# A shared-expert split moved one attention step on, and three neighbours of it reordered, in an attention and mixture-of-experts kernel

## The chip, the cores and the metric

The kernel runs on one core of a Trainium2 chip. The metric is device time in microseconds (us), lower is better. The five engines are TensorE (PE in the rows; PEld is its weight load), VectorE (DVE), ScalarE (ACT), GpSimd (POOL) and SyncE (SP, which here only issues DMAs).

## The reference

One layer of linear attention with decay over 4096 tokens of width 512, a layer norm, then a mixture of 64 experts (top 6, at most 128 slots each) plus one shared expert, and a second layer norm:

```python
q, k, v = split(x @ w_qkv);  q, k = elu(q) + 1, elu(k) + 1
running_kv, running_ksum = decay_scan(k * v), decay_scan(k)      # s = decay * s + x over the tokens
x1 = layernorm(x + (q * running_kv / sum(q * running_ksum)) @ w_out)
scores = softmax(x1 @ gate_w.T);  w, e = top_k(scores, 6)
routed = sum over the chosen experts of w * ((silu(g) * u) @ down_proj[e]),  g, u = split(x1 @ gate_up_proj[e])
shared = silu(x1 @ shared_gate_w.T) * (x1 @ shared_up_w.T) @ shared_down_w.T
out = layernorm(x1 + routed + shared)
```

Every float32 factor is written as a high part (rounded, made by ScalarE) and a low part (the rest, made by VectorE as the difference), and TensorE computes three products for one.

## The kernel before

**Attention.** The tokens are cut into eight blocks of 512 (`it`), and each block takes four steps (`c`), one for each 128 of the width. Every engine runs its own list of the same steps, written out by hand, and semaphores join them. In a step (it, c) TensorE projects k, v and q, ScalarE makes the exponentials and relus (`e`, `relu`), VectorE makes `phi_k`, the two scans `run_k` and `run_kv`, `phi_q` and `qk`. Mixed in is the work of the block before: four quotients (`spread` on TensorE, `divide` on VectorE, `split_att` for their high and low parts), four `out_rows` (the output projection, one for each 128-token tile), `add_x1` with the norm's statistics (`mv`), three small GpSimd instructions for the norm (`norm`), and `apply_x1` on ScalarE. A later step turns the tile (`turn_x1`, `copy_turned`), computes its gate logits, picks the top six (`top`, `route`, `place`) and, on GpSimd, writes the tile's slots with six indirect DMAs (`scatter`). Tiles 24 to 27 get their output rows in block 7; the tiles from `LAST` = 28 on get theirs in a tail after the last step. Tiles up to 26 are scattered, the last five are counted into the table by matmuls (`table_add`).

**The shared expert** is cut into units of one chain of matmuls each (gate, up, then pairs of down rows); the first run in the tail, the others between the experts and behind them. Before the first unit its operands must be split: the turned x1 of block 0 (`split_x1t(0)`: four casts `x1t_hi` on ScalarE, four differences `x1t_lo` on VectorE, from `x1t_stage`, which SyncE loads in step (7, 0)), the up weights (`su_hi`, `su_lo`), the gate weights (`sg_hi`, `sg_lo`) and the down weights (`sd_hi`, `sd_lo`). The semaphore `shared_split` counts the low parts that are ready; the down units and two expert loads of SyncE wait for its last value.

**What sets the order** around the change is the written order of each engine's list. An engine that waits holds up everything behind it in its own list.

Of the kernel before, what the change touches and what calls it, by code (L numbers as in the profile page):

```python
# [7 lines left out]
F32 = mybir.dt.float32  # L8
# [3 lines left out]
ALU = mybir.AluOpType  # L12
# [33 lines left out]
def build(nc, x, x_t, w_qkv, w_out, decay_param, gate_t, w_gu, w_down, sg_t, su_t, sd_t, out):  # L46
# [5 lines left out]
    NB = T // BT  # L52
    NJ = BT // P
    NT = T // P
    KC = D // P
    SC = SI // P
# [264 lines left out]
    with ExitStack() as ctx:  # L321
# [93 lines left out]
        def _(sp):  # L415
# [151 lines left out]
            store_turned(LAST - 1)  # L567
            load_xres(NB - 1, 3)
            store_score(LAST - 1)
            sp.wait_ge(shared_split, 3)  # L570
            for e in range(2):
                load_down(e)
            for i in range(LAST, NT):
# [59 lines left out]
        def _(act):  # L633
# [112 lines left out]
            def unit():  # L746
                b, part = divmod(unit_at[0], UNITS)
                unit_at[0] += 1
                if part < 2 * SC:
                    c = part // 2  # L750
                    n = SC * b + c
                    if part % 2 == 0:
                        act.wait_ge(g_mm, n + 1)
                        if n:
                            act.wait_ge(silu_done, n)
                        ps = proj_ps[(unit_take(b) + part) % 3]
                        act.activation(tanh_s[:, :], ps[:, :], ACT.Tanh, scale=0.5).then_inc(tanh_done, 1)
                        if part == 0 and b + 1 < NB:
                            load_x1t(b + 1)
                    else:  # L760
                        act.wait_ge(hid_s_done, n + 1)
                        if b:
                            act.wait_ge(down_mm, NJ * b)
                        act.copy(hid_hi[:, c, :], hid_s[:, :]).then_inc(hid_hi_done, 1)
                    return
                if part == 2 * SC and b + 1 < NB:
                    split_x1t(b + 1)
                pair = part - 2 * SC
                for j in (2 * pair, 2 * pair + 1) if b < EARLY else ():
                    act.wait_ge(down_mm, NJ * b + j + 1)  # L770
                    if b == 0 and j == 0:
                        act.wait_ge(heads_mm, NB)
                    if b == 1 and j == 0:
                        act.wait_ge(rest_mm, NT)
                        act.wait_ge(out_mm, NT)
                        act.wait_ge(table_done, TABLE_JOINED)
                    if b >= len(shared_rows) and j == 0:
                        act.wait_ge(shared_out[b - len(shared_rows)], 16)
                    act.copy(shared_rows[b % len(shared_rows)][:, j, :], proj_ps[rows_take[b, j] % 3][:, :]).then_inc(rows_copied, 1)
# [48 lines left out]
            for it in range(NB):  # L828
                for c in range(KC):
                    step(it, c)  # L830
                    if (it, c) == (NB - 1, 0):
                        split_x1t(0)
                    if (it, c) == (NB - 1, 1):
                        split_shared(0, "u", su_hi, su_stage)
                    if (it, c) == (NB - 1, 2):
                        split_shared(1, "g", sg_hi, sg_stage)
# [11 lines left out]
            divided[0] += 2  # L848
            split_att()
            copy_logits(LAST - 2)  # L850
            unit()
            divided[0] += 2
            split_att()
            scale_score(LAST - 2)
            unit()
            apply_x1(LAST - 1)
            unit()
# [108 lines left out]
        def _(dve):  # L966
# [286 lines left out]
            def split_shared(hi, lo, view):  # L1253
                dve.tensor_tensor(lo[:, :, :], view[:, :, :], hi[:, :, :].bitcast(F32), ALU.subtract).then_inc(shared_split, 1)

            def step(it, c):
                tile, before_tile = tile_of(it, c), tile_of(it, c - 1)
                s = it * KC + c
# [4 lines left out]
                    numerator(s - 1)  # L1263
                if s and it + 1 < NB:
                    x_low(it + 1, c)
                dve.wait_ge(phi_parts, 2 * s + 1)
                if s:
                    dve.wait_ge(run_kv_done, s)
# [36 lines left out]
                mix(it, c, 1)  # L1305
                if c == 0 and it:
                    rden_low(it - 1)
                if (it, c) == (NB - 1, KC - 2):
                    dve.wait_ge(shared_hi_done, 1)
                    split_shared(su_hi, su_lo, su_stage)  # L1310
                if (it, c) == (NB - 1, KC - 1):
                    dve.wait_ge(shared_hi_done, 2)
                    split_shared(sg_hi, sg_lo, sg_stage)
# [46 lines left out]
            divide(NB - 1, 1)  # L1360
            place(LAST - 3)
            split_att()
            top(LAST - 2)
            route(LAST - 2)
            unit()
            divide(NB - 1, 2)
            divide(NB - 1, 3)
            split_att()
            place(LAST - 2)
            unit()  # L1370
            add_x1(LAST)
            unit()
            dve.wait_ge(shared_hi_done, 3)
            split_shared(sd_hi, sd_lo, sd_stage)
            add_x1(LAST + 1)
            top(LAST - 1)
            route(LAST - 1)
            add_x1(LAST + 2)
            place(LAST - 1)
            add_x1(LAST + 3)  # L1380
# [244 lines left out]
        def _(pe):  # L1625
# [123 lines left out]
            def unit():  # L1749
                b, part = divmod(unit_at[0], UNITS)  # L1750
                unit_at[0] += 1
                if part < 2 * SC:
                    c = part // 2
                    take = unit_take(b) + part
                    cols = slice(c * P, (c + 1) * P)
                    w_hi, w_lo = (su_hi, su_lo) if part % 2 else (sg_hi, sg_lo)
                    pe.wait_ge(shared_split, 2)
                    pe.wait_ge(x1t_lo_done, KC * (b + 1))
                    pe.wait_ge(*freed[take - 3])
                    products = []  # L1760
                    for k in range(KC):
                        products += three(w_hi[:, k, cols], w_lo[:, k, cols], x1t_hi[:, k, :], x1t_lo[:, k, :])
                    chain(proj_ps[take % 3][:, :], products).then_inc(u_mm if part % 2 else g_mm, 1)
                    return
                pair = (2 * (part - 2 * SC), 2 * (part - 2 * SC) + 1)
                pe.wait_ge(shared_split, 3)
                for late_chunk in (False, True):
                    for j in pair:
                        take = rows_take[b, j]
                        tok = slice(j * P, (j + 1) * P)  # L1770
                        chunks = [SC - 1] if late_chunk else range(SC - 1)
                        if not late_chunk:
                            pe.wait_ge(*freed[take - 3])
                        pe.wait_ge(hid_lo_done, SC * b + (SC if late_chunk else SC - 1))
                        products = []
                        for c in chunks:
                            products += three(hid_hi[:, c, tok], hid_lo[:, c, tok], sd_hi[:, c, :], sd_lo[:, c, :])
                        mm = chain(proj_ps[take % 3][:, :], products, first=not late_chunk, final=late_chunk)
                        if late_chunk:
                            mm.then_inc(down_mm, 1)  # L1780
# [150 lines left out]
```

## Time and profile before

| | |
|---|---|
| three runs | 949.8, 950.09, 954.65 us (median 950.09) |
| profiled execution | 952.04 us, its span 949.6 us |
| PE busy | 919.3 us, 97% of the span |
| DVE, ACT, POOL busy | 683.2, 499.7, 463.9 us |
| mean granted TensorE clock | 0.993 |

Busy time is an average over the whole span; the attention steps end near 411 us, the tail runs to about 475 us, the experts follow up to about 880 us and the last norm closes the kernel. Times in the rows count from the start of the span, so a row of one engine can be laid beside a row of another.

### The profile page before, as it was taken

What the parts mean: (1) busy time and instruction counts of PE and PEld (TensorE: products, weight loads), DVE (VectorE), ACT (ScalarE), POOL (GpSimd) and SP (SyncE); (2) the same over time, 40 slices, a digit from 0 to 9 for tenths busy, and PEclk for the clock granted to TensorE, in tenths of its full rate; (3) what the DMA queues carried; (4) which work ended last, traced back from release to release, by engine and by line L of the source; (5) the groups of instructions that cost most, each with busy time, mean ns of one, the idle gap of its engine ahead of it and who ended that gap; (6) DMA issues with size and microseconds to landing.
All of it is one profiled execution on the core that took longest, in us unless ns stands there. A gap on an engine that the chain in (4) does not pass through costs nothing. (4 is left out here: it accounts for less than half of the span.)

```text
span 949.6 us, 15173 instructions
## 1 busy us (share of the span) xinstructions
PE 919.3 (97%) x4626; PEld 728.9 (77%) x4626; DVE 683.2 (72%) x1248; ACT 499.7 (53%) x1015; POOL 463.9 (49%) x540
## 2 busy tenths in 40 slices
PE   8999999999999998998999999999989999999996
PEld 7788888878887886786787767777767777777875
DVE  7996878889797975887776556575656665636776
ACT  5543535344443433443556655666645666545775
POOL 2002456665656654577135455554454644433564
PEclk9999999999999998999999999999999999999999
DMA  6244635334343515176569999999999999969972
GB/s 209 88 154 122 176 87 166 108 115 124 126 126 92 157 59 184 55 239 222 167 201 298 304 321 312 321 314 308 312 303 300 320 319 302 319 116 392 385 255 112
DMA packets 114190, 203.91 MB, mean 215 GB/s; under 512 B 18496, under 2 KB 56384, under 8 KB 113088
## 3 DMA queue, kind: packets, MB, share of 16 engines
q1 hardware_dynamic: 93584, 159.87, 51.0%
q0 software_dynamic: 19520, 35.75, 16.4%
q10 hardware_dynamic: 1008, 7.34, 2.1%
q8 instruction: 38, 0.62, 0.3%
q14 instruction: 40, 0.33, 0.1%
HBM read 143.03 MB, written 59.88 MB: 214 GB/s over the span
## 5 line engine op out<-in xcount | busy, mean ns | idle before, releaser
L1531 POOL DMA_INDIRECT slot_table<-tokens,slot_of x162 | 179.3, 1107 | 94.4 <-issue 50.3
L1573 POOL DMA_INDIRECT acc_rows<-eo,table_sb x64 | 111.4, 1740 | 167.8 <-ACT eo L889 135.7
L1628 PE MATMUL bank<-x_hi,wqkv_hi 128*128 128x512 f32 x384 | 153.0, 398 | 0.9 <-DVE wqkv_lo L973 0.9
L1628 PE MATMUL bank<-x_lo,wqkv_hi 128*128 128x512 f32 x384 | 150.9, 393 | 0.0
L1628 PE MATMUL bank<-x_hi,wqkv_lo 128*128 128x512 f32 x384 | 150.8, 393 | 0.0
L1400 DVE TENSOR_TENSOR wgu_lo<-wgu,wgu_hi 128x1536 fp32r<-128x1536 f32 x64 | 112.5, 1760 | 42.8 <-ACT wgu_hi L883 42.8
L1628 PE MATMUL bank<-wdn,hid_et 96*128 96x512 f32 x256 | 121.9, 598 | 7.9 <-ACT hid_et L925 7.9
L1562 POOL DMA_INDIRECT xg<-x_rows,table_sb x64 | 78.2, 1222 | 39.1 <-DVE table_sb L1134 19.8
L883 ACT CAST wgu_hi<-wgu 128x1536 fp32r<-128x1536 f32 x64 | 94.5, 1477 | 1.0 <-DMA wgu<-w_gu 0.5
L1628 PE MATMUL bank<-wgu_hi,xgt_hi 128*128 128x384 f32 x256 | 91.6, 358 | 0.0
L1628 PE MATMUL bank<-wgu_hi,xgt_lo 128*128 128x384 f32 x256 | 86.0, 336 | 0.0
L1628 PE MATMUL bank<-wgu_lo,xgt_hi 128*128 128x384 f32 x256 | 85.9, 336 | 0.0
L1628 PEld LDWEIGHTS bank<-x_hi,wqkv_hi 128*128 128x128 f32 x384 | 72.8, 190 | 17.0 <-issue 1.4
L1628 PEld LDWEIGHTS bank<-x_hi,wqkv_lo 128*128 128x128 f32 x384 | 72.5, 189 | 15.7
L1628 PEld LDWEIGHTS bank<-x_lo,wqkv_hi 128*128 128x128 f32 x384 | 72.7, 189 | 15.3
L656 ACT ACTIVATE e<-bank 128x512 f32<-128x512 f32 x64 | 38.0, 594 | 78.0 <-PE bank L1628 77.8
L1628 PEld LDWEIGHTS bank<-wdn,hid_et 96*128 96x128 f32 x256 | 43.5, 190 | 40.4 <-issue 30.8
L1427 DVE SCALAR_TENSOR_TENSOR silu_e<-tanh_e,bank 128x192 f32<-128x192 f32 x64 | 22.6, 354 | 71.5 <-ACT tanh_e L913 71.5
L1515 POOL TENSOR_SCALAR rstd<-mv 128x1 f32<-128x1 f32 x32 | 9.7, 302 | 123.6 <-DVE mv L1000 122.3
L889 ACT ACTIVATE eo<-bank,xg 128x512 f32<-128x512 f32 x64 | 44.3, 692 | 43.1 <-DMA acc_rows<-eo,table_sb 37.8
L1628 PE MATMUL bank<-wout_hi,att_hi 128*128 128x512 f32 x128 | 52.3, 408 | 4.8 <-issue 3.3
L913 ACT ACTIVATE tanh_e<-bank 128x192 f32<-128x192 f32 x64 | 21.2, 331 | 67.6 <-PE bank L1628 67.5
(183 smaller groups left out, 2146.0 us busy)
## 6 DMA issues: line engine op xcount, KB each, us to landing
wgu<-w_gu SPq DMA_DIRECT2D x64, 768.0 KB, 8.4
wdn<-w_down SPq DMA_DIRECT2D x64, 384.0 KB, 8.1
xres<-x SPq DMA_DIRECT2D x32, 256.0 KB, 3.0
x_turned<-x1t SPq DMA_DIRECT2D x32, 256.0 KB
x_rows<-x SPq DMA_DIRECT2D x32, 256.0 KB, 3.2
acc_rows<-x SPq DMA_DIRECT2D x32, 256.0 KB, 2.8
fin<-acc_rows SPq DMA_DIRECT2D x8, 1024.0 KB, 11.9
odd<-acc_rows SPq DMA_DIRECT2D x8, 1024.0 KB, 13.9
```

The costliest lines, as they stand in the source:

```text
L656: act.activation(e_sb[q][:, :], ps[:, :], ACT.Exp)
L883: act.copy(wgu_hi[e % 2][:, :, :], wgu_buf[e % NG][:, :, :]).then_inc(wgu_hi_done, 1)
L889: act.activation(eo[eo_slot[e]][:, :], eo_ps[:, :], ACT.Copy, scale=xg[e % NXG][:, D + e:D + e + 1]).then_inc(eo_done, 1)
L913: act.activation(tanh_e[:, :], gu_ps[e % 2][:, 0:I], ACT.Tanh, scale=0.5).then_inc(tanh_e_done, 1)
L1400: dve.tensor_tensor(wgu_lo[e % NG][:, :, :], wgu_buf[e % NG][:, :, :], wgu_hi[e % 2][:, :, :].bitcast(F32), ALU.subtract).then_inc(wgu_lo_ ...
L1427: dve.scalar_tensor_tensor(out=silu_e[:, :], in0=tanh_e[:, :], scalar=1.0, in1=ps[:, 0:I], op0=ALU.add, op1=ALU.mult).then_inc(silu_e_done, 1)
L1515: pool.tensor_scalar(rstd[i][:, :], mv[i][:, 1:2], EPS_NORM, None, ALU.add).then_inc(norm_done, 1)
L1531: pool.indirect_dma_start(table_dram, bass.IndirectOffsetOnAxis(slot_of[:, i, k:k + 1], 0), tokens[:, i:i + 1], None, bounds_check=SLOTS - ...
L1562: pool.indirect_dma_start(xg[e % NXG][:, :], None, x1_dram, bass.IndirectOffsetOnAxis(table_sb[:, e:e + 1], 0), bounds_check=T - 1, oob_is ...
L1573: pool.indirect_dma_start(acc_dram[e % 2], bass.IndirectOffsetOnAxis(table_sb[:, e:e + 1], 0), eo[eo_slot[e]][:, :], None, bounds_check=T ...
L1628: mm = pe.matmul(out_ap, a, b, start=first and i == 0, stop=final and i == len(products) - 1)
```

## The change

Five edits in the last attention block and the tail. `split_x1t(0)` on ScalarE stands behind step (7, 1) instead of (7, 0). The low part of the up weights on VectorE stands ahead of `phi_k` in step (7, 2) instead of ahead of `phi_q`. In the tail the last two quotients of block 7 come ahead of a shared unit, on VectorE and ScalarE. The low part of the down weights is made in three instructions of a third each instead of one: the first ahead of `top(26)`, the others behind `route(27)`. The waits on the last value of `shared_split` count to 5 instead of 3.

```diff
@@ SyncE
-            sp.wait_ge(shared_split, 3)
+            sp.wait_ge(shared_split, 2 + SC)
             for e in range(2):
                 load_down(e)
@@ ScalarE
                     step(it, c)
-                    if (it, c) == (NB - 1, 0):
+                    if (it, c) == (NB - 1, 1):
                         split_x1t(0)
-                    if (it, c) == (NB - 1, 1):
                         split_shared(0, "u", su_hi, su_stage)
...
             copy_logits(LAST - 2)
-            unit()
             divided[0] += 2
             split_att()
             scale_score(LAST - 2)
+            unit()
             unit()
             apply_x1(LAST - 1)
@@ VectorE
+            def split_down(c):
+                dve.wait_ge(shared_hi_done, 3)
+                dve.tensor_tensor(sd_lo[:, c, :], sd_stage[:, c, :], sd_hi[:, c, :].bitcast(F32), ALU.subtract).then_inc(shared_split, 1)
...
                     x_low(it + 1, c)
+                if (it, c) == (NB - 1, KC - 2):
+                    dve.wait_ge(shared_hi_done, 1)
+                    split_shared(su_hi, su_lo, su_stage)
                 dve.wait_ge(phi_parts, 2 * s + 1)
...
-                if (it, c) == (NB - 1, KC - 2):
-                    dve.wait_ge(shared_hi_done, 1)
-                    split_shared(su_hi, su_lo, su_stage)
                 if (it, c) == (NB - 1, KC - 1):
...
             split_att()
+            split_down(0)
             top(LAST - 2)
             route(LAST - 2)
-            unit()
             divide(NB - 1, 2)
             divide(NB - 1, 3)
             split_att()
+            unit()
             place(LAST - 2)
             unit()
             add_x1(LAST)
             unit()
-            dve.wait_ge(shared_hi_done, 3)
-            split_shared(sd_hi, sd_lo, sd_stage)
             add_x1(LAST + 1)
             top(LAST - 1)
             route(LAST - 1)
+            for c in range(1, SC):
+                split_down(c)
             add_x1(LAST + 2)
@@ TensorE
-                pe.wait_ge(shared_split, 3)
+                pe.wait_ge(shared_split, 2 + SC)
```

ScalarE's list at the end of step (7, 0) and the start of step (7, 1), before; `e_82` and `relu` are what `phi_k` of step (7, 1) needs, `x1t_142` is the turned tile 22:

```order
L716 ACTIVATE neg_max<-top_v 128x1
L721 ACTIVATE e_route,e_sum<-logits,neg_max 128x64
L735 CAST x1t_hi<-x1t_stage 128x512 x4
L691 ACTIVATE score_131<-e_route,r_sum 128x64
L656 ACTIVATE e_82<-bank 128x512
L661 ACTIVATE relu<-bank 128x512
L701 COPY x1t_142<-bank 128x512
```

The end of step (7, 1) and the start of step (7, 2) on ScalarE with the change:

```order
L716 ACTIVATE neg_max<-top_v 128x1
L721 ACTIVATE e_route,e_sum<-logits,neg_max 128x64
L735 CAST x1t_hi<-x1t_stage 128x512 x4
L727 CAST su_hi<-su_stage 128x1536
L691 ACTIVATE score_130<-e_route,r_sum 128x64
L656 ACTIVATE e_82<-bank 128x512
L661 ACTIVATE relu<-bank 128x512
```

The four casts now stand directly ahead of `su_hi`, 13 rows further on.

VectorE's list at the start of step (7, 2) with the change (before, `su_lo` stood between `run_kv` and `phi_q`; `num_113` is the numerator of step (7, 1)):

```order
L1014 TENSOR_TENSOR num_113<-phi_q,run_kv 128x512
L1253 TENSOR_TENSOR su_lo<-su_stage,su_hi 128x1536
L1275 SCALAR_TENSOR_TENSOR phi_k<-e_82,relu 128x512
L988 TENSOR_TENSOR att_lo<-num_110,att_hi 128x512
L1021 TENSOR_TENSOR num_111<-num_111,bank 128x512
L1291 SCALAR_TENSOR_TENSOR run_k<-decay,state,phi_k 128x512
```

Everything of the step on VectorE now stands behind `su_lo`, and `su_lo` behind `su_hi` of ScalarE.

VectorE's list in the tail, before, from the second shared unit (`hid_s`, `hid_lo`) to the output rows of tile 28, with the two last quotients `num_108` and `num_109`:

```order
L1244 SCALAR_TENSOR_TENSOR hid_s<-silu_s,bank 128x512
L1249 TENSOR_TENSOR hid_lo<-hid_s,hid_hi 128x512
L1022 TENSOR_TENSOR num_108<-num_108,bank 128x512
L1022 TENSOR_TENSOR num_109<-num_109,bank 128x512
L989 TENSOR_TENSOR att_lo<-num_108,att_hi 128x512
L989 TENSOR_TENSOR att_lo<-num_109,att_hi 128x512
L1143 TENSOR_TENSOR before_end<-any_choice_133,bank 128x64
```

The same place with the change:

```order
L1021 TENSOR_TENSOR num_108<-num_108,bank 128x512
L1021 TENSOR_TENSOR num_109<-num_109,bank 128x512
L988 TENSOR_TENSOR att_lo<-num_108,att_hi 128x512
L988 TENSOR_TENSOR att_lo<-num_109,att_hi 128x512
L1243 SCALAR_TENSOR_TENSOR hid_s<-silu_s,bank 128x512
L1248 TENSOR_TENSOR hid_lo<-hid_s,hid_hi 128x512
L1142 TENSOR_TENSOR before_end<-any_choice_133,bank 128x64
```

The unit has moved behind the quotients and their low parts.

## Rows read from the trace of the kernel before

**Rows 1.** Busy time of each engine by stretch, with granted clock and DMA share.

```profile
core 0: us, PE busy (x) PEld busy (x) DVE busy (x) ACT busy (x) POOL busy (x), PEclk, DMA share, GB/s
370.00:373.80 3.80, 0.37 (x3) 0.10 (x1) 0.47 (x1) 3.77 (x8) 1.13 (x2) 0.97 0.01 0
373.80:380.40 6.60, 6.58 (x20) 5.51 (x21) 6.53 (x10) 2.60 (x7) 0.00 (x0) 0.50 0.82 243
500.00:850.00 350.00, 342.08 (x1620) 262.48 (x1619) 206.82 (x275) 211.49 (x341) 177.57 (x120) 1.00 1.02 301
...
708.00:712.00 4.00, 4.00 (x11) 2.49 (x10) 2.23 (x2) 1.63 (x2) 3.12 (x3) 0.57 1.06 299
```

**Rows 2.** Timeline at step (7, 0)'s end: start us, length us, engine, instruction, [idle before].

```profile
363.83 0.65 SPq L543 DMA_DIRECT2D x1t_stage<-x_turned  x1
369.90 2.18 ACT L735 CAST x1t_hi<-x1t_stage 128x512 fp32r<-128x512 f32 x4 [5.72 <-DMA x1t_stage<-x_turned]
371.99 0.34 ACT L691 ACTIVATE score<-e_route,r_sum 128x64 f32<-128x64 f32 x1
373.82 1.97 PE L1628 MATMUL bank<-gate_sb,x1t 128*128 128x64 f32 x8 [3.45 <-ACT x1t L701]
```

**Rows 3.** Timeline of PE: the same two places of block 6 and of block 7.

```profile
300.51 0.65 PE L1684 MATMUL bank<-qk,head_cols 128*32 128x128 f32 x16
329.10 0.48 PE L1628 MATMUL bank<-wout_hi,att_hi 128*128 128x512 f32 x1
...
352.79 0.64 PE L1684 MATMUL bank<-qk,head_cols 128*32 128x128 f32 x16
...
388.07 0.48 PE L1628 MATMUL bank<-wout_hi,att_hi 128*128 128x512 f32 x1
```

**Rows 4.** Timeline of POOL, DVE, ACT and PE, tile 24's norm to tile 30's turn.

```profile
395.97 0.59 POOL L1515 TENSOR_SCALAR rstd<-mv 128x1 f32<-128x1 f32 x1 [5.91 <-DVE mv L1000]
434.79 0.97 POOL L1531 DMA_INDIRECT slot_table<-tokens,slot_of  x1 [0.30 <-issue]
435.94 1.75 DVE L1254 TENSOR_TENSOR sd_lo<-sd_stage,sd_hi 128x1536 fp32r<-128x1536 f32 x1
436.07 2.47 POOL L1531 DMA_INDIRECT slot_table<-tokens,slot_of  x1 [0.30 <-issue]
450.23 0.54 POOL L1519 TENSOR_SCALAR shift<-mv,rstd 128x1 f32<-128x1 f32 x1
450.81 0.81 ACT L677 ACTIVATE x<-x,shift,rstd 128x512 f32<-128x512 f32 x1 [2.13 <-POOL shift L1519]
451.68 0.33 PE L1723 MATMUL bank<-ident,x 128*128 128x128 f32 x1 [0.74 <-ACT x L677]
```

**Rows 5.** Timeline of ACT and DVE in steps (6, 1) and (7, 2).

```profile
322.76 0.19 ACT L721 ACTIVATION_READ_ACCUMULATOR e_route<-logits,neg_max 128x1 f32 x1
...
382.20 1.47 ACT L727 CAST su_hi<-su_stage 128x1536 fp32r<-128x1536 f32 x1
384.91 0.69 DVE L1269 SCALAR_TENSOR_TENSOR phi_k<-e,relu 128x512 f32<-128x512 f32 x1 [1.46 <-ACT relu L661]
390.42 1.73 DVE L1254 TENSOR_TENSOR su_lo<-su_stage,su_hi 128x1536 fp32r<-128x1536 f32 x1
392.06 0.68 DVE L1318 SCALAR_TENSOR_TENSOR phi_q<-e,relu 128x512 f32<-128x512 f32 x1
395.69 0.18 DVE L1000 BATCH_NORM_AGGREGATE mv<-stats 128x2 f32<-128x6 f32 x1
```

**Rows 6.** Timeline of PE and DVE in the tail.

```profile
422.24 1.29 DVE L989 TENSOR_TENSOR att_lo<-num,att_hi 128x512 fp32r<-128x512 f32 x2 [0.23 <-ACT att_hi L672]
429.29 0.47 PE L1628 MATMUL bank<-wout_hi,att_hi 128*128 128x512 f32 x1 [1.48 <-DVE num L1022]
438.40 0.47 PE L1628 MATMUL bank<-wout_hi,att_hi 128*128 128x512 f32 x1 [1.43 <-issue]
```

**Rows 7.** Timeline of PE among the experts.

```profile
569.36 0.70 PE L1628 MATMUL bank<-wdn,hid_et 96*128 96x512 f32 x1 [1.85 <-ACT hid_et L925]
706.92 0.70 PE L1628 MATMUL bank<-wdn,hid_et 96*128 96x512 f32 x1 [3.08 <-ACT hid_et L925]
```

## The prediction

> **What bounds the kernel now.** I read the busy time by stretch first, then the waits of the last attention block, then the timelines of all engines beside each other. TensorE bounds: in the long expert stage it is busy 342.08 of 350 us [rows 1], so time comes off only where TensorE stands idle or runs slowly, and a later stage keeps a gain made ahead of it. The windows show one such place that stands out: from 370.0 to 373.8 TensorE works 0.37 us, and from 373.8 to 380.4 it is busy throughout at a granted clock of 0.50, the lower level of 1.2 GHz, after having stood idle [rows 1].
>
> The timeline says why. SyncE issues the load of `x1t_stage` at 363.83; ScalarE stands at `x1t_hi` in its list and waits 5.72 us for it, until 369.90. Behind it in the list wait the score, `e`, `relu` and the copy of turned tile 22, and TensorE's gate matmuls wait 3.45 us for that copy [rows 2].
>
> What this costs, idle and slow clock together, can be read against the block before, which has the same list and no stall. In block 6 the output rows begin 28.59 us behind the head sums (329.10 - 300.51), in block 7 35.28 us behind them (388.07 - 352.79) [rows 3]. The difference, 6.69 us, is the price of the stall.
>
> **The second limit is GpSimd.** From the norm of tile 24 (395.97) to that of tile 30 (shift ends at 450.77) the only idle time ahead of a GpSimd instruction in its timeline is the fraction of a microsecond between two issues; ahead of the first it waited 5.91 us for VectorE's `mv`. Tile 30's `apply_x1` waits 2.13 us for this chain and TensorE's turn of tile 30 waits 0.74 us for that [rows 4]. So whatever TensorE, VectorE or ScalarE gain between 396 and 451 us is handed back at 451.7, and the stage begins earlier only if `mv` of tile 24 does.
>
> **The change part by part.**
>
> *The split of x1t one step on.* The wait goes: the load landed at 369.90, and ScalarE now comes to it at the end of step (7, 1). That end, in block 6, is 322.95 [rows 5]; with the blocks' distance of 52.28 us (352.79 - 300.51) it is 375.2, so 5 us are to spare. Worth 6.7 us. Then what the four casts delay in their new place: the next instruction starts 2.09 us behind the first of them (371.99 - 369.90) [rows 2], and `su_hi` takes 1.47 [rows 5]. It ends at 375.2 + 2.1 + 1.5 = 378.8.
>
> *The up weights' low part at the head.* VectorE gets there at about 376 and waits for `su_hi`. Everything of step (7, 2) is queued behind it: `phi_k`, two low parts of quotients, both scans, then `add_x1(24)` with `mv`. The instruction takes 1.64 us to the next start (392.06 - 390.42), so `phi_k` starts at 380.4. From `phi_k` to `mv` were 10.78 us (395.69 - 384.91) without a pause in the timeline, 1.64 of which was `su_lo` itself [rows 5]; 9.14 are left, and `mv` starts at 389.55. It stood at 395.69: 6.1 us earlier. So these two edits together are worth 6.1, and 0.6 of the 6.7 stays in the ScalarE and VectorE queues. TensorE feels it as a short wait ahead of the gate of tile 23 and the output rows of tile 24. If `su_hi` were not late, moving `su_lo` would cost nothing, since it is the same work in the same chain.
>
> *The last quotients ahead of the unit.* They remove the unit's 2 us from ahead of them, and with it TensorE's 1.48 us wait at 429.29 [rows 6]. The unit's own parts come later, ahead of `place(26)`, and `apply_x1(27)` behind it on ScalarE, so TensorE waits a few tenths at the turn of tile 27 instead. *The down weights in three pieces.* The 1.75 us that stand ahead of `add_x1(29)`, and behind them TensorE's 1.43 us wait [rows 6], go; the pieces cost 1.8 us (three of 0.6, from two low parts in 1.29) [rows 6], the first in a wait of VectorE for logits, the other two ahead of `add_x1(30)`, whose matmuls then still run. For TensorE both edits save some 2 to 3 us by 440 us, and the GpSimd chain takes them back at the turns of tiles 28 and 30. I count them at nothing for the end of the kernel; bounds 0 and 3.
>
> *What the pieces do to GpSimd.* One scatter beside `sd_lo` took 2.47 us where the one ahead of it took 0.97 [rows 4]: the chain lost 1.5 us while VectorE ran that one long instruction. With pieces that loss can fall away or come back in part, since two of them now run about where tile 28's and 29's norms stand. Bounds: 1.5 and 0; I take 0.8, the middle, because each piece is a third as long.
>
> The Trainium skill, SBUF — State Buffer, section Who interferes with whom, says that a VectorE instruction with two SBUF inputs and a GpSimd instruction that reads SBUF share an interface, and that the loser waits for the whole instruction of the other. The 2.47 us row agrees; by that rule the worst wait behind one piece is one piece's length, so that the sum would lie between the two bounds just given. The same rule speaks against moving `su_lo`: it falls beside tile 21's scatters. That costs the end nothing, since GpSimd then idles before tile 24's `mv`.
>
> *The counts.* Waiting for 5 instead of 3 concerns the down units and two loads. The down units begin at 456.8, far behind the last piece at about 439, and the loads at 443.18 stand behind tile 27's score in SyncE's list. Nothing.
>
> Sum: 6.1 + 0.8 = 6.9 us. The profiled execution took 952.04 us, so 945.1 for its like; the median of the runs is 950.09, 1.95 less than that one, which makes 943.2.
>
> **The rivals.**
>
> 1. *A new idle stretch lets the clock fall.* TensorE gets ahead of GpSimd in the tail, so its wait of 0.74 at the turn of tile 30 grows to about 2 us, and one of 1 to 1.6 us appears ahead of tile 28's. Idle of 3.08 us ahead of 706.92 [rows 7] was followed by a stretch at 0.57 [rows 1]; 1.85 ahead of 569.36 [rows 7] is nearer to 2, and the stretch behind it ran at full clock. A fall costs half of the slow stretch, 3.3 us [rows 1]: 946.5. Chance 0.10.
> 2. *GpSimd is not the limit that I take it for*, and the 2 to 3 us of the tail edits come through: 943.2 - 2.5 = 940.7. The 0.74 at 451.68 speaks against, the roughness of GpSimd's spans for. Chance 0.12.
> 3. *The queue of step (7, 2) or the expert stage gives back half*, because `su_hi` comes later than counted or the DMA queues, with a share of 1.02 there [rows 1], pace the experts: 943.2 + 3.4 = 946.6. TensorE's 342 us of 350 speak against. Chance 0.14.
> 4. *The change does nothing*: the stall moves with the cast or is absorbed later; 950. The load has 5 us to spare. Chance 0.03.
> 5. *Slower.* VectorE now waits for `su_hi` ahead of `phi_k`, and ScalarE reaches `su_hi` only behind the load of `x1t_stage`, so a late load would stop both. Each microsecond of `su_hi` beyond 378.8 goes to the end one for one. The gain is used up when it ends at 378.8 + 6.9 = 385.7, for which the load must land near 382, 18 us behind its issue instead of 6; at 391 the time would be 943.2 + 12.2 = 955.4. Nothing in the rows is near that. Chance 0.03.
>
> **How the numbers follow.** 0.58 is left for the forecast of 943.2, with its own range of 941.5 to 945.3. What a measurement of this kernel can tell from no change is about 0.5%, 4.75 us, so faster means below 945.34. Faster: the forecast's 0.58 nearly whole (0.57), rival 2 (0.12) and the better edge of rivals 1 and 3 (0.05), 0.74. Slower: 0.03. Within: 0.23. The range reaches from rival 2 and a little below it, 939.5, to above rivals 1 and 3, 948; rivals 4 and 5 lie outside.
>
> **What the changed profile would show.** ScalarE's 5.72 us wait for `x1t_stage` gone, TensorE busy at clock 1.00 from 365 to 385, VectorE waiting about 2.5 us for `su_hi` ahead of `su_lo`, output rows of tile 24 near 382.3, `mv` of tile 24 near 389.6, no 2.47 us scatter, tile 30's shift at about 443.8 and TensorE idle for 1 to 2 us ahead of its turn. The prediction is wrong if `mv` of tile 24 moves by less than 5 us, or if the time from it to the turn of tile 30 changes by more than 2 us, or if the distance from there to the end differs.

## The result, and the profile after

The changed kernel takes 947.86 us, the median of 15 runs (941.76 to 952.18); the kernel before took 951.13 us in 15 runs of the same series (947.6 to 954.95). The ratio is 0.996, with a 95% interval of 0.9944 to 0.9976: 3.8 us less by that ratio (the two medians are 3.3 apart, the means 4.2), where the prediction had 6.9. The profiled execution took 947.28 us with a span of 945.2 (before 952.04 and 949.6).

Busy time by stretch in the profile after, with the granted clock and the DMA share:

```profile
core 0: us, PE busy (x) PEld busy (x) DVE busy (x) ACT busy (x) POOL busy (x), PEclk, DMA share, GB/s
...
370.00:373.80 3.80, 3.80 (x22) 3.28 (x22) 3.73 (x7) 1.99 (x6) 1.52 (x2) 1.00 1.02 285
373.80:380.40 6.60, 6.60 (x33) 5.09 (x31) 4.16 (x12) 6.02 (x13) 4.56 (x4) 1.00 0.29 82
440.00:445.00 5.00, 2.94 (x29) 2.30 (x27) 2.77 (x10) 0.99 (x5) 4.06 (x7) 1.00 0.95 312
445.00:450.00 5.00, 4.27 (x14) 3.60 (x15) 1.56 (x7) 3.33 (x9) 0.96 (x3) 0.66 0.09 27
...
500.00:850.00 350.00, 341.83 (x1624) 262.60 (x1623) 204.86 (x273) 207.88 (x336) 170.50 (x118) 1.00 1.02 298
```

The hole of [rows 1] is closed: TensorE works through from 370.0 to 380.4 at full clock. A new one stands 70 us later, where TensorE is busy 2.94 of 5 us, and the 5 us behind that run at a mean clock of 0.66. The expert stage is as it was.

The timeline after, all engines, first at the stage's head and then in the tail:

```profile
352.68 1.08 PE L1688 MATMUL bank<-qk,head_cols 128*32 128x128 f32 x32
364.31 0.35 ACT L691 ACTIVATE score<-e_route,r_sum 128x64 f32<-128x64 f32 x1 [0.23 <-DVE r_sum L1094]
378.51 1.76 DVE L1253 TENSOR_TENSOR su_lo<-su_stage,su_hi 128x1536 fp32r<-128x1536 f32 x1 [2.32 <-ACT su_hi L727]
380.73 1.10 PE L1632 MATMUL bank<-gate_sb,x1t 128*128 128x64 f32 x8 [0.19 <-ACT x1t L701]
382.33 0.47 PE L1632 MATMUL bank<-wout_hi,att_hi 128*128 128x512 f32 x1 [0.49 <-DVE num L1021]
389.30 0.18 DVE L999 BATCH_NORM_AGGREGATE mv<-stats 128x2 f32<-128x6 f32 x1
389.57 0.58 POOL L1519 TENSOR_SCALAR rstd<-mv 128x1 f32<-128x1 f32 x1 [5.52 <-DVE mv L999]
...
425.95 0.47 PE L1632 MATMUL bank<-wout_hi,att_hi 128*128 128x512 f32 x1 [0.76 <-issue]
428.16 0.69 DVE L1248 TENSOR_TENSOR hid_lo<-hid_s,hid_hi 128x512 fp32r<-128x512 f32 x1 [0.69 <-ACT hid_hi L764]
428.29 1.41 POOL L1535 DMA_INDIRECT slot_table<-tokens,slot_of  x1 [0.30 <-issue]
431.60 1.27 DVE L1257 TENSOR_TENSOR sd_lo<-sd_stage,sd_hi 128x512 fp32r<-128x512 f32 x2
432.03 0.89 POOL L1523 TENSOR_SCALAR shift<-mv,rstd 128x1 f32<-128x1 f32 x1
433.82 0.66 PE L1727 MATMUL bank<-ident,x 128*128 128x128 f32 x4 [0.99 <-ACT x L677]
435.98 0.95 DVE L1121 TENSOR_TENSOR slot_is<-slot_no,position 128x768 bf16<-128x768 f32 x1
436.06 1.71 POOL L1535 DMA_INDIRECT slot_table<-tokens,slot_of  x1 [0.31 <-issue]
443.08 0.95 DVE L1121 TENSOR_TENSOR slot_is<-slot_no,position 128x768 bf16<-128x768 f32 x1
443.33 1.13 POOL L1521 TENSOR_TENSOR rstd<-rstd,minus_half 128x1 f32<-128x1 f32 x1
444.56 0.27 POOL L1523 TENSOR_SCALAR shift<-mv,rstd 128x1 f32<-128x1 f32 x1
444.86 0.81 ACT L677 ACTIVATE x<-x,shift,rstd 128x512 f32<-128x512 f32 x1 [4.01 <-POOL shift L1523]
445.73 1.12 PE L1727 MATMUL bank<-ident,x 128*128 128x128 f32 x4 [2.79 <-ACT x L677]
478.34 0.33 PE L1632 MATMUL bank<-wgu_hi,xgt_hi 128*128 128x384 f32 x1
```

The score at 364.31 starts with a wait of 0.23 us where `x1t_hi` had waited 5.72 [rows 2]. Output rows of tile 24 begin at 382.33 instead of 388.07 [rows 3] and `mv` follows at 389.30 instead of 395.69 [rows 5]. In the tail the waits of 1.48 and 1.43 us [rows 6] have become one of 0.76, and TensorE's wait at the turn of tile 30, 0.74 before [rows 4], is 2.79. There GpSimd has no 2.47 us scatter any more, but one of 1.71 and a `rstd` of 1.13, each beside a VectorE instruction with two inputs. (One scatter of 2.36 us has come up at 378.75, beside `su_lo`; it lies ahead of the 5.52 us in which GpSimd waits for `mv`, so it costs nothing, as the prediction said.)

**A ruler.** From one profile to the next the head sums of block 7 begin at 352.68 to 354.95 us, and the way from the first expert matmul to the end takes 462.0 to 469.9, a spread with no order that follows the edits. So the profiles are compared by distances within each: from the head sums of block 7 (`bank<-qk,head_cols`) to `mv` of tile 24, from there to the turn of tile 30, and from the turn to the first expert matmul (`bank<-wgu_hi,xgt_hi`; row above for after). In the kernel before that first expert matmul is this row of TensorE's timeline:

```profile
482.44 0.41 PE L1628 MATMUL bank<-wgu_hi,xgt_hi 128*128 128x384 f32 x1
```

| kernel | sums to mv 24 | mv 24 to turn 30 | turn 30 to experts | sum | against before |
|---|---|---|---|---|---|
| before | 42.90 | 55.99 | 30.76 | 129.65 | |
| after | 36.62 | 56.43 | 32.61 | 125.66 | -3.99 |

From the first expert matmul to the end of the span it is 467.1 before and 466.9 after, so the two spans differ by what is made ahead of the experts. The difference of 4 us there agrees with the timed runs.

### The profile page after: what moved, and what is told of

Read it like the earlier page. It is cut to its first block and busy times, and to the rows that moved or that the text cites. A ratio compares the mean times of both kernels' runs of the same rounds, so it can differ in the third digit from the quotient of the medians.

```text
span 945.2 us, 15175 instructions
## 1 busy us (share of the span) xinstructions
PE 918.1 (97%) x4626; PEld 727.5 (77%) x4626; DVE 683.3 (72%) x1250; ACT 499.5 (53%) x1015; POOL 460.9 (49%) x540
## 5 line engine op out<-in xcount | busy, mean ns | idle before, releaser
L1566 POOL DMA_INDIRECT xg<-x_rows,table_sb x64 | 74.3, 1162 | 41.3 <-DVE table_sb L1133 22.0
```

The costliest lines, as they stand in the source:

```text
L1566: pool.indirect_dma_start(xg[e % NXG][:, :], None, x1_dram, bass.IndirectOffsetOnAxis(table_sb[:, e:e + 1], 0), bounds_check=T - 1, oob_is ...
```

## The experiments

All kernels of one series ran on one chip beside the kernel before, whose median was 950.32 us in the first series, 958.56 in the second and 951.79 in the third. The distances are put together in a table behind the first and the third.

### First series: parts of the change

**1. Only the casts of x1t moved.** The kernel before with this edit:

```diff
-                    if (it, c) == (NB - 1, 0):
-                        split_x1t(0)
                     if (it, c) == (NB - 1, 1):
+                        split_x1t(0)
                         split_shared(0, "u", su_hi, su_stage)
```

> The kernel before with one edit: the four casts of the turned x1 stand behind step (7, 1) instead of (7, 0). Theory A (the stall's removal is worth 6 us at tile 24's statistics, and what TensorE gains later in the tail is taken back by the GpSimd chain and by a fall of the clock in the wait that opens there): VectorE's phi_k of step (7, 2) starts when its relu is ready, near 379.9, and 10.8 us later come tile 24's statistics, near 390.7, 5.0 us earlier than before; the GpSimd chain from there to tile 30's shift takes 54.8 us as before, the wait ahead of the turn of tile 30 stays under 1.3 us, the clock stays at 1.00, and 4.5 to 5.5 us are kept to the end, a ratio of 0.994 to 0.9955. Rival B (the gain is real but about 2 us of it are lost in the expert stage): the profile shows the same shift at 450 us but less at the end, a ratio of 0.997.

Measured: 946.31 us (12 runs), ratio 0.9959 (0.9933 to 0.9985). `mv` of tile 24 came at 390.57, as theory A had it; that the clock would hold did not come true. By stretch, and in TensorE's timeline:

```profile
385.00:390.00 5.00, 2.75 (x13) 1.99 (x12) 4.86 (x10) 1.12 (x6) 0.00 (x0) 1.00 0.00 0
390.00:395.00 5.00, 5.00 (x15) 3.97 (x16) 4.31 (x12) 2.34 (x4) 3.50 (x5) 0.66 0.25 59
```

```profile
389.91 0.47 PE L1627 MATMUL bank<-wout_hi,att_hi 128*128 128x512 f32 x1 [2.25 <-issue]
446.92 0.66 PE L1722 MATMUL bank<-ident,x 128*128 128x128 f32 x4 [0.21 <-ACT x L677]
```

Here `su_lo` is still in VectorE's way in the middle of step (7, 2), and TensorE waits 2.25 us ahead of the output rows of tile 25; the clock falls behind that wait. The trace names no releaser for it, but the matmul starts 0.1 us after VectorE's `add_x1(24)` has read its bank (389.12 to 389.81). `mv` of tile 24, and with it GpSimd's norm, comes 1.2 us later than with both edits (37.84 us behind the head sums against 36.60).

**2. Both edits at the head.** Edit 1, and `su_lo` ahead of `phi_k`:

```diff
+                if (it, c) == (NB - 1, KC - 2):
+                    dve.wait_ge(shared_hi_done, 1)
+                    split_shared(su_hi, su_lo, su_stage)
                 dve.wait_ge(phi_parts, 2 * s + 1)
...
-                if (it, c) == (NB - 1, KC - 2):
-                    dve.wait_ge(shared_hi_done, 1)
-                    split_shared(su_hi, su_lo, su_stage)
```

> The kernel before with two edits: the casts behind step (7, 1), and the up weights' low part ahead of phi_k in step (7, 2). Theory A: tile 24's statistics near 389.6 as in the changed kernel, 6.1 us earlier than before, the GpSimd chain 54.8 us, TensorE not ahead of it in the tail, so the wait ahead of the turn of tile 30 is near 0.7 us and the clock stays at 1.00: 6 us kept to the end, ratio 0.9935, which is better than the whole change. Rival B: no better than the whole change, 0.996.

Measured: 944.49 us (7 runs), ratio 0.9928 (0.9899 to 0.9956). TensorE's timeline:

```profile
424.00 0.47 PE L1627 MATMUL bank<-wout_hi,att_hi 128*128 128x512 f32 x1 [1.48 <-DVE num L1021]
433.10 0.47 PE L1627 MATMUL bank<-wout_hi,att_hi 128*128 128x512 f32 x1 [1.45 <-issue]
446.39 0.66 PE L1722 MATMUL bank<-ident,x 128*128 128x128 f32 x4 [0.74 <-ACT x L677]
477.45 0.33 PE L1627 MATMUL bank<-wgu_hi,xgt_hi 128*128 128x384 f32 x1
```

This is the tail of before with its three waits, 1.48, about 1.4 and 0.74, moved forward as a whole. The two edits at the head bring 6.0 us up to the experts, and the timed gain, 0.72% or 6.8 us, agrees.

**3. Only the edits of the tail.** The quotients ahead of the unit and `sd_lo` in pieces, as in the diff of the change, with the head as before.

> The changed kernel with its two head edits undone: only the quotients ahead of the unit and the down weights in three pieces. Theory A: the stall at 370 is as before; in the tail TensorE gets 2 to 3 us ahead, the GpSimd chain from tile 24's statistics to tile 30's shift takes 55.3 us instead of 54.8, TensorE waits near 2.8 us ahead of the turn of tile 30, and where the clock falls in that wait 1.7 us are lost: ratio 1.000 to 1.003, no gain at all. Rival B: the tail edits bring the 2 us that TensorE gains, ratio 0.998, and the loss is elsewhere.

Measured: 951.91 us (12 runs), ratio 1.0013 (0.999 to 1.0036). By stretch, and TensorE's timeline:

```profile
446.00:451.00 5.00, 3.09 (x29) 2.41 (x27) 2.87 (x11) 0.98 (x4) 4.12 (x6) 0.99 0.97 320
451.00:456.00 5.00, 4.11 (x12) 3.44 (x13) 1.57 (x7) 3.47 (x9) 1.05 (x3) 0.50 0.05 14
456.00:461.00 5.00, 5.00 (x37) 3.95 (x37) 2.84 (x9) 0.00 (x0) 0.00 (x0) 0.82 0.44 153
```

```profile
432.09 0.47 PE L1633 MATMUL bank<-wout_hi,att_hi 128*128 128x512 f32 x1 [0.76 <-issue]
451.89 1.11 PE L1728 MATMUL bank<-ident,x 128*128 128x128 f32 x4 [2.79 <-ACT x L677]
```

The wait of 2.79 us belongs to the tail's edits, whatever the head does, and here the half clock behind it lasted 6.83 us.

**4. The wait filled.** The changed kernel with 22 transposes into a bank that nobody reads, ahead of the turn of tile 30, so that TensorE works while it waits.

```diff
+    FILL = 22
...
+                    if i + 1 == LAST + 2:
+                        pe.wait_ge(x1t_done, i + 1)
+                        for _ in range(FILL):
+                            pe.transpose(turn_ps[:, 0:P], ident[:, :], ident[:, :])
```

> The changed kernel with 22 more 128x128 transposes of the identity into the turning bank ahead of the turn of tile 30, about 2.2 us of TensorE work in the place where it waits 2.8 us; nothing reads them. Theory A: the turn of tile 30 starts where it did, near 445.7, but the clock stays at 1.00 behind it, and 1.7 us more are kept: ratio to the kernel before 0.994 instead of 0.996. Rival B: the same as the changed kernel, 0.996, or 2 us worse if the transposes were in the way.

Measured: 946.99 us (12 runs), ratio 0.997 (0.9946 to 0.9993). By stretch, and TensorE's timeline:

```profile
445.00:450.00 5.00, 4.62 (x38) 3.60 (x36) 1.85 (x9) 3.47 (x9) 1.32 (x4) 1.00 0.08 18
```

```profile
446.17 0.66 PE L1728 MATMUL bank<-ident,x 128*128 128x128 f32 x4 [0.39 <-ACT x L678]
476.98 0.35 PE L1633 MATMUL bank<-wgu_hi,xgt_hi 128*128 128x384 f32 x1
```

The turn comes when it came, since GpSimd sets it, but the clock stays at 1.00 and the four transposes take 0.66 us instead of 1.12. From the turn to the experts it is 30.81 us instead of 32.61: the half clock costs 1.8 us. The timed ratio does not show it: 5.79 us would be 0.9939, just outside the interval, which lies on that of the changed kernel. So the price rests on the profiles alone; how much of it the timed runs get back stays open.

| kernel | sums to mv 24 | mv 24 to turn 30 | turn 30 to experts | sum | against before | timed ratio |
|---|---|---|---|---|---|---|
| 1, casts alone | 37.84 | 56.35 | 30.77 | 124.96 | -4.69 | 0.9959 |
| 2, head | 36.60 | 55.98 | 31.06 | 123.64 | -6.01 | 0.9928 |
| 3, tail | 42.19 | 56.45 | 33.57 | 132.21 | +2.56 | 1.0013 |
| 4, after, filled | 36.61 | 56.44 | 30.81 | 123.86 | -5.79 | 0.997 |

### Second series: GpSimd's order and the whole piece

**5. The norm of tile 30 ahead of the scatters of tile 26**, in the changed kernel:

```diff
             norm(LAST + 1)
-            scatter(LAST - 2)
             norm(LAST + 2)
+            scatter(LAST - 2)
             norm(LAST + 3)
```

> The changed kernel with one exchange on GpSimd: the norm (shift) of tile 30 stands ahead of the index scatters of tile 26 instead of behind them. Theory A, GpSimd's chain is the limit at the turn of tile 30: the shift of tile 30 ends near 436 to 440 instead of 444.83, the 2.79 us wait ahead of TensorE's turn of tile 30 is gone, the granted clock stays at 1.00 there, and the way from the shared MLP's moving of tile 24 to the first expert matmul falls from 89.04 us to about 85 (2.8 of wait and 1.7 of half clock less): ratio to the kernel before about 0.9915. Rival B, something else ends at the same time (ScalarE's copy or the late scatters ahead of the expert gathers): the way stays at 87 to 89 and the ratio at 0.996.

Measured: 954.83 us (12 runs), ratio 0.996 (0.9927 to 0.9993).

**6. The down weights' low part whole again**, at its old place, in the changed kernel:

```diff
             split_att()
-            split_down(0)
...
             unit()
+            dve.wait_ge(shared_hi_done, 3)
+            split_shared(sd_hi, sd_lo, sd_stage)
             add_x1(LAST + 1)
             top(LAST - 1)
             route(LAST - 1)
-            for c in range(1, SC):
-                split_down(c)
```

> The changed kernel with the low part of the down weights as one VectorE instruction at its old place; the quotients stay moved. Theory A, the pieces bring GpSimd nothing: a scatter beside that one instruction takes about 2.4 us again, the chain from the norm of tile 24 to the shift of tile 30 measures 54.8 us instead of 55.3, TensorE's 1.4 us wait for the low attention part comes back and the wait at the turn of tile 30 shrinks by as much, so the clock may hold: the first expert matmul at 476 to 478.3, ratio to the kernel before 0.993 to 0.996. Rival B, the forecast's term (pieces relieve GpSimd by 0.8 us): the chain grows to 56 us and the first expert matmul comes at 479 or later, ratio 0.997.

The counts on `shared_split` go back to 3 with it.

Measured: 952.11 us (12 runs), ratio 0.9943 (0.9909 to 0.9977). That lies in theory A's range, but the interval holds rival B's 0.997 as well.

**7. The norms of tiles 28 and 30 in between the scatters**, in the changed kernel, where `scatter(i, first, final)` issues part of the six:

```diff
-            scatter(LAST - 3)
+            scatter(LAST - 3, 0, 3)
             norm(LAST)
+            scatter(LAST - 3, 3)
             norm(LAST + 1)
-            scatter(LAST - 2)
+            scatter(LAST - 2, 0, 2)
             norm(LAST + 2)
+            scatter(LAST - 2, 2)
             norm(LAST + 3)
```

> The changed kernel with the norms of tiles 28 and 30 moved in between the scatters of tiles 25 and 26 on GpSimd (three scatters, norm 28, the rest; norm 29; two scatters, norm 30, the rest; norm 31). Theory A, GpSimd's order sets TensorE's waits at the turns of tiles 28 and 30: both waits (0.99 and 2.79 us) and the half clock (1.7 us) are gone, up to 5.5 us less than the changed kernel, first expert matmul near 473, ratio to the kernel before 0.989 to 0.990. Rival B, the norms of tiles 29 and 31 or the last scatters are late instead: first expert matmul at 476 or later, ratio 0.994 to 0.996.

Measured: 946.91 us (11 runs), ratio 0.9896 (0.9863 to 0.993).

**8. That order alone**, in the kernel before.

> The kernel before with only that order on GpSimd (norms of tiles 28 and 30 in between the scatters), its stall at the turn of tile 23 kept. Theory A, GpSimd's chain runs continuously in the kernel before too but TensorE hardly waits for it (0.74 us ahead of the turn of tile 30): it gains 0.7 to 1.5 us, ratio 0.998 to 1.0. Rival B, TensorE's quotient waits (1.48 and 1.43 us) were hidden costs of the same chain and the gain is 3 us or more: ratio 0.997 or less.

Measured: 956.69 us (12 runs), ratio 0.9988 (0.9956 to 1.0021).

The ratios of kernels 7 and 8 are those of theory A, that of kernel 5 is rival B's, though the interval of kernel 8 reaches into its rival's range too. But all four profiles of this series have waits of ScalarE between 406 and 431 us that no profile of the first series has, and the kernel before was 8 us slower on this chip as well. ScalarE in kernel 7:

```profile
411.77 0.58 ACT L701 COPY x1t<-bank 128x512 f32<-128x512 f32 x1 [3.65 <-remote]
416.15 0.60 ACT L757 ACTIVATE tanh_s<-bank 128x512 f32<-128x512 f32 x1 [2.65 <-remote]
424.92 0.21 ACT L714 COPY logits<-bank 128x64 f32<-128x64 f32 x1 [3.91 <-remote]
```

Kernel 8, with the head of before, has the same three at 417.39, 421.76 and 430.58 (3.51, 2.64 and 3.96 us). Behind them the output rows of tile 28 come late, `mv` of tile 28 too, and in kernels 5 and 6 GpSimd stands idle 5.00 and 4.63 us ahead of that norm, so that its order no longer decides anything. These profiles don't answer the question that kernels 5 and 6 were made for. Kernels 5 and 7 were run again beside the changed one.

### Third series: the changed kernel and GpSimd's orders side by side

**9. The changed kernel again**, unchanged.

> The changed kernel once more, beside the two that follow. In the profiles of the kernels with a new GpSimd order, TensorE's turn of tiles 26 to 28 came 3 to 6 us later than in the profiles taken earlier, with waits of ScalarE of 3.65, 2.65 and 3.91 us between 408 and 425 us that the trace gives to nothing it knows. Theory A, those waits come from the chip or the moment, not from the order: here either no kernel of this row of runs shows them or all do. Rival B, the order makes them: they are missing here and there in the two others. Ratio to the kernel before 0.996.

Measured: 947.52 us (12 runs), ratio 0.9955 (0.9927 to 0.9983). TensorE's timeline:

```profile
435.83 0.66 PE L1727 MATMUL bank<-ident,x 128*128 128x128 f32 x4 [1.01 <-ACT x L677]
447.73 0.66 PE L1727 MATMUL bank<-ident,x 128*128 128x128 f32 x4 [2.79 <-ACT x L677]
480.42 0.33 PE L1632 MATMUL bank<-wgu_hi,xgt_hi 128*128 128x384 f32 x1
```

The same two waits as in the first profile after, to 0.02 us, and half clock behind the second again (0.85 from 445 to 450 us, 0.81 in the next five). None of the four profiles of this series has the waits of the second: they come from that chip or moment, not from the order.

**10. Kernel 7 again.**

> The changed kernel with the norms of tiles 28 and 30 in between the scatters of tiles 25 and 26, once more. Theory A, GpSimd's order sets the waits at the turns of tiles 28 and 30: against the changed kernel beside it the distance from the shared MLP's moving of tile 24 to the first expert matmul is 3 to 5 us shorter, no half clock between 440 and 460 us, ratio to the kernel before 0.990. Rival B, the better ratio seen before came from the chip's state: the ratio is 0.994 to 0.996 and the distance the same.

Measured: 939.95 us (6 runs), ratio 0.9901 (0.9868 to 0.9934). By stretch, then the timeline of TensorE and GpSimd:

```profile
440.00:445.00 5.00, 5.00 (x40) 4.15 (x40) 3.79 (x15) 2.59 (x9) 3.84 (x6) 1.00 0.86 276
445.00:450.00 5.00, 5.00 (x41) 4.16 (x40) 3.63 (x13) 2.51 (x7) 0.27 (x1) 1.00 0.50 167
```

```profile
427.43 0.23 POOL L1519 TENSOR_SCALAR rstd<-mv 128x1 f32<-128x1 f32 x1 [0.18 <-DVE mv L999]
434.16 0.47 PE L1634 MATMUL bank<-wout_hi,att_hi 128*128 128x512 f32 x1 [0.31 <-issue]
438.36 0.26 POOL L1523 TENSOR_SCALAR shift<-mv,rstd 128x1 f32<-128x1 f32 x1
473.45 0.41 PE L1634 MATMUL bank<-wgu_hi,xgt_hi 128*128 128x384 f32 x1
```

TensorE waits at no turn any more. Between 435 and 458 us its timeline shows no idle time, the clock is 1.00 throughout, and the shift of tile 30 ends at 438.62, 6.2 us earlier than after (444.83). This is the fastest of the kernels.

**11. Kernel 5 again.**

> The changed kernel with only the norm of tile 30 exchanged with the scatters of tile 26, once more. Theory A, without the waits that stood in the earlier profile the wait of 2.79 us at the turn of tile 30 is gone and the one of 0.99 us at the turn of tile 28 stays: distance to the first expert matmul 3 to 4.5 us shorter than in the changed kernel beside it, ratio to the kernel before 0.991 to 0.993. Rival B, the late scatters of tile 26 give it back at the gathers: first expert matmul as in the changed kernel, ratio 0.996.

Measured: 942.52 us (7 runs), ratio 0.9916 (0.9886 to 0.9945). The wait of 1.01 us at the turn of tile 28 is left, that at the turn of tile 30 is gone, with the fall of the clock. From the turn to the experts it is 30.76 us, as in the kernel before, so the late scatters of tile 26 give nothing back: theory A.

**12. The head's edits and GpSimd's new order, without the tail's edits.** Kernel 2 with the diff of kernel 7.

> The kernel before with the two edits at the stage's head and the new GpSimd order, without the quotients moved and without the pieces. Theory A, the tail's two edits bring nothing once GpSimd is ahead: TensorE keeps its two waits for the quotients and the low attention part (1.48 and 1.45 us) but none at the turns: ratio 0.991 to 0.993, 1 to 3 us over the kernel with all four parts. Rival B, the tail's edits are worth nothing even then (the quotients' waits end something that waits anyway): ratio as with all parts, 0.990.

Measured: 946.08 us (10 runs), ratio 0.9943 (0.9921 to 0.9966), a little over the range of theory A. TensorE's timeline:

```profile
424.06 0.47 PE L1629 MATMUL bank<-wout_hi,att_hi 128*128 128x512 f32 x1 [1.48 <-DVE num L1021]
433.16 0.47 PE L1629 MATMUL bank<-wout_hi,att_hi 128*128 128x512 f32 x1 [1.43 <-issue]
476.47 0.33 PE L1629 MATMUL bank<-wgu_hi,xgt_hi 128*128 128x384 f32 x1
```

| kernel | sums to mv 24 | mv 24 to turn 30 | turn 30 to experts | sum | against before | timed ratio |
|---|---|---|---|---|---|---|
| 9, after again | 36.62 | 56.45 | 32.69 | 125.76 | -3.89 | 0.9955 |
| 10, norms between | 36.62 | 52.89 | 30.73 | 120.24 | -9.41 | 0.9901 |
| 11, norm 30 first | 36.62 | 53.50 | 30.76 | 120.88 | -8.77 | 0.9916 |
| 12, without the tail's edits | 36.62 | 55.07 | 30.95 | 122.64 | -7.01 | 0.9943 |

Kernels 12 and 10 differ by the tail's edits alone, with GpSimd out of the way: 2.40 us up to the experts, nearly all of it between `mv` and the turn. With GpSimd's old order the same edits lose 2.02 us (after against kernel 2). GpSimd's new order by itself is worth 1.00 (kernel 12 against kernel 2), both together 3.40: each needs the other. The timed runs point the same way both times. In this series five of kernel 10's six runs are faster than the fastest of kernel 12's ten; in the first series the ratio is 0.9928 without the tail's edits where with them it was 0.996, with intervals that overlap. In size they are not as exact as the distances: the medians of kernels 9, 12 and 10 are 947.52, 946.08 and 939.95 us, steps of 1.4 and 6.1 where the distances have 3.12 and 2.40.

## Why the prediction was right and where it failed

The direction was right, and so was the mechanism of the gain. The size was not: 3.8 us instead of 6.9, in the sum of the ruler 3.99 = 6.28 - 0.44 - 1.85. The measured 947.86 us lies just inside the upper edge of the range, 948, but not below the 945.34 that the prediction called faster, to which it gave 0.74. Two steps failed, both about the tail: the 0.8 us that GpSimd's chain was to gain, and the tail's edits "at nothing".

**The head's edits, forecast 6.1, measured 6.28** from the head sums to `mv` (42.90 to 36.62), and 6.01 for kernel 2 up to the experts. Each sign stood where it was said: VectorE's wait for `su_hi` 2.32 us (about 2.5), output rows of tile 24 at 382.33 (382.3), `mv` at 389.30 (389.6). Comparing block 7 with block 6 gave the price of the stall rightly. It is hardly a price of the clock, though. Kernels 3 and 8 kept the stall, with 2.75 and 3.26 us of idle, and the clock stayed at 1.00 behind it; from the head sums to `mv` they took 42.19 and 42.71 us, only 0.7 and 0.2 less than the 42.90 with the half clock. TensorE, faster there, waited 2.23 and 2.25 us instead of 1.22 ahead of the output rows of tile 25: ScalarE's and VectorE's queues were late, and it merely used up the room behind them.

**GpSimd is the second limit, as said.** Its chain from the norm of tile 24 to the shift of tile 30 took 55.26 us after (389.57 to 444.83) and 54.80 before (395.97 to 450.77), with no pause above 0.43 us between two instructions. Kernels 10 and 11 show it by moving two norms and one.

**The step "I take 0.8, the middle" was wrong.** The pieces were to give back 0.8 of the 1.5 us that one scatter lost beside `sd_lo`. The 2.47 us scatter did vanish, but the chain grew by 0.46, a miss of 1.26 us. The term itself was sized about rightly: 1.50 us fell away, and beside the pieces only the shift of tile 28 was stretched, to 0.89 us where it took 0.27 before, which leaves 0.88. But the forecast looked for costs only beside the pieces. The tail's edits moved all of VectorE's work in time, and other instructions of it came to lie on the chain: `hid_lo` at 428.16 on a scatter of 1.41 us (0.44 lost), `slot_is`, 0.95 us long, at 435.98 on the scatter of 1.71 (0.74 lost) and at 443.08 on the `rstd` of 1.13 (0.56 lost). In the kernel before, `hid_lo` began in the middle of a scatter that took its usual 0.97, the first `slot_is` 0.29 us behind the start of one that took 1.05, and the second stretched the norm of tile 31, behind the limit. These 1.74 us, less 0.4 us of small losses of before that fell away, make up the miss. Kernel 3 has the same 55.28, kernel 2 the same 54.80, so the growth belongs to the tail's edits. That the stretched instructions wait for VectorE is read from the rows side by side; no run moved `slot_is` or `hid_lo` alone. How much of the shift in time is the pieces' and how much the quotients' stays open, since the profile of kernel 6 has the waits of the second series, and its ratio, 0.9943, cannot be told from 0.996.

The Trainium skill, SBUF — State Buffer, section Who interferes with whom, has the loser wait for the other's whole instruction. The trace agrees: the scatters of 2.47 and 1.71 us end 0.85 and 0.84 us after the VectorE instructions beside them, 1.75 and 0.95 us long. And by that rule it was every two-input instruction of VectorE beside the chain that had to be counted, in its new place, not only the one that was cut up.

**Counting the tail's edits "at nothing for the end of the kernel; bounds 0 and 3" was wrong, and so was the 0.10 for rival 1.** TensorE was ready for the turn of tile 30 at 442.94 instead of 450.94, and met a chain that was only 5.94 us earlier (444.83 against 450.77). Its wait rose by 8.00 - 5.94, from 0.74 to 2.79. Rival 1 named the place and had about 2 us; 1.26 us less of chain would have made it 1.5 at the least. The clock then fell, in all three profiles that have this wait (after, kernel 9, kernel 3). Rival 1 sized the fall at 3.3 us, which is half of the longer kind of slow stretch; after and in kernel 9 it lasted 3.41 us, and kernel 4 puts its price at 1.8. So the tail's edits did not cost nothing but 2.3 us here: 0.44 in the chain and 1.85 in the clock (2.0 against kernel 2). The bounds excluded a loss, and no row gave a reason for that. That rival 1's 946.5 comes near the measured time is in part luck: its fall was too dear by some 1.5 us, and the chain's 1.26 us were missing. Two of the signs that the prediction set itself say the same: TensorE's idle time ahead of the turn was to be 1 to 2 us and was 2.79, and the distance from there to the end was to stay and grew by 1.6 us (1.85 up to the experts).

**Why rival 1 was held unlikely.** One wait of 1.85 us [rows 7] with full clock behind it was taken for a rule. Over all fourteen profiles, between 350 and 940 us, TensorE has 16 waits of 1.8 to 2.3 us, and 7 of them were followed within 3 us by a stretch at the lower clock; of 15 waits of 2.7 us and more, 13 were. A single row is no threshold. Seen from there, with a wait forecast near 2 us, rival 1 should have had a chance near a half, and the range should have been centred higher.

**Rival 2** (940.7) fell: nothing of the tail's 2 to 3 us came through while GpSimd set the turns. The 2 to 3 us themselves were right: with GpSimd ahead they are 2.40. **Rivals 3 and 4** fell too: the expert stage took what it took before (467.1 and 466.9; one pair proves little where the profiles spread by 8 us, but the timed 3.8 us agree with the 3.99 made ahead of it), and the stall did not move. **Rival 5** was far off, since `su_hi` ended in time.

## What to carry to other kernels

A gain on the bounding engine that ends in a wait for a second limit is not worth zero: it widens a gap, and a gap can cost the clock. So look whom the faster engine meets next and move that work first; here a few lines that let two norms pass some index scatters turned a loss of 2.0 us into a gain of 2.4 and brought the kernel from 0.996 to 0.990. When work is moved in time on VectorE, check what it newly lies beside on GpSimd, not only what is taken away.

## What the runs showed of the hardware that was not expected

- The clock: waits of the same length were followed by a fall to half in one profile and not in another. Two waits of 2.25 and 2.23 us at the same instruction (kernels 1 and 3) had a clock of 0.66 over the next 5 us and of 1.00; waits of 2.75 and 3.26 us at the gate of tile 23 were followed by full clock and one of 3.45 by half [rows 1, 2]. Behind the same wait of 2.79 us the slow stretch lasted 3.41 us twice and 6.83 us once.
- GpSimd: the pow of `rstd` takes 0.57 us alone and 1.13 beside a VectorE instruction of 0.95 us; an index scatter takes 0.97 alone, 1.71 beside the same, 2.47 beside one of 1.75 us [rows 4].
- One series of four kernels showed three waits of ScalarE, of 2.64 to 4.71 us and at the same three instructions in all four, for which the trace names no releaser, and a kernel before that took 8 us more. Two of the four, run again in the third series, had none of them. What they are stays open. For one of the two the ratio to the kernel before of the same series held (0.9896 and 0.9901); for the other, where the waits lie ahead of the very norm that was moved, it was 0.996 and then 0.9916, with intervals that overlap.
